# Cross-attention and a top-2 expert layer on one core: the opening put in another order, and the end done in two halves of the tokens

## What is computed

```python
x = x + attention(layernorm(x), ctx, ctx, mask)   # x 1 x 1024 x 128, ctx 1 x 6404 x 128, 16 heads of 8
    # q, k, v with weights and biases; scores / sqrt(8); where(mask, lowest float, scores); softmax; Wo, bo
x = x + ffn(layernorm(x))
    # logits = x @ gate_w.T; softmax; top 2 of 8 experts;
    # per expert h = gelu(x @ w1 + b1), y = h @ w2 + b2; sum of the two, weighted by their probabilities
# mask[b, s, s2] is True for keys 0 .. len-1 of every row: most keys are hidden, those behind len are seen
```

## Time and profile before

| | us |
|---|---|
| three runs | 343.9, 342.21, 339.49 |
| their median | 342.21 |
| the profiled execution | 344.7 |
| its span, first to last instruction | 343.0 |
| PE busy | 269.3 (79%) |
| ACT busy | 233.3 (68%) |
| DVE busy | 175.9 (51%) |
| POOL busy | 64.7 (19%) |

### The profile page before, as it was taken

One profiled execution on the slowest core, in us unless ns is written; L12 is line 12 of the kernel. 1 busy time (PEld: TensorE's weight loads), 2 busy tenths in 40 slices (PEclk: granted clock), 3 DMA queues, 4 the chain that ended last, 5 costly groups with the idle time before them and its releaser, 6 DMA issues.

```text
span 343.0 us, 6176 instructions
## 1 busy us (share of the span) xinstructions
PE 269.3 (79%) x1852; PEld 130.0 (38%) x1852; DVE 175.9 (51%) x423; ACT 233.3 (68%) x365; POOL 64.7 (19%) x109
## 2 busy tenths in 40 slices
PE   0488974899999989899999999796476049999950
PEld 0444554413222212121222212124275049999940
DVE  4939984042345353544445353635791316677722
ACT  3449806356799999999999999892588015555520
POOL 8920002000000000000000002101027703444440
PEclk9999965579999999999999999999989559999995
DMA  6999872010010101001010101059801170101104
GB/s 192 375 263 330 336 162 59 0 28 13 2 38 2 38 11 27 16 22 25 13 36 3 38 11 27 11 172 371 152 9 57 47 193 24 33 31 33 33 31 183
DMA packets 33891, 29.57 MB, mean 86 GB/s; under 512 B 15344, under 2 KB 29192, under 8 KB 33744
## 3 DMA queue, kind: packets, MB, share of 16 engines
q1 hardware_dynamic: 32304, 26.41, 26.8%
q0 software_dynamic: 1568, 2.93, 3.0%
HBM read 21.62 MB, written 7.45 MB: 85 GB/s over the span
## 4 chain that ended last, share of the span: by engine, by line
PE 31%; issue 26%; DVE 16%; ACT 14%; SPq 5%; DMA 4%; ACTq 1%; DVEq 1%; POOL 1%; POOLq 0%
PE bank L1188 7%; ACT w2T L955 7%; ACT arenaB L955 7%; PE bank L1177 6%; PE bank L1311 5%; DVE arenaC L501 4%; SPq L301 4%; PE bank L1174 3%; PE bank L1319 3%; DVE arenaB L864 2%; PE bank L1107 2%; SPq L274 1%; DMA arenaA<-ys_dram 1%; PE bank L1023 1%; DMA x_sb<-in_x_dram 1%
## 5 line engine op out<-in xcount | busy, mean ns | idle before, releaser
L683 DVE TENSOR_TENSOR arenaA<-bank,arenaA 128x512 f32<-128x512 f32 x80 | 55.2, 690 | 84.7 <-PE bank L1188 84.6
L955 ACT ACTIVATE arenaB<-bank 128x1024 f32<-128x1024 f32 x80 | 77.8, 1022 | 12.1 <-PE bank L1177 10.2
L955 ACT ACTIVATE w2T<-bank 128x1024 f32<-128x1024 f32 x80 | 76.8, 1028 | 4.9 <-PE bank L1177 3.8
L1177 PE MATMUL bank<-qS,keys 64*128 64x512 bf16 x324 | 63.8, 392 | 10.0 <-ACT w2T L955 5.0
L985 ACT ACTIVATE mask_u<-bank,arenaB 128x128 f32<-128x128 f32 x92 | 26.2, 368 | 38.9 <-PE bank L1311 38.9
L1177 PEld LDWEIGHTS bank<-qS,keys 64*128 64x128 bf16 x324 | 15.5, 93 | 97.5 <-ACT w2T L955 45.0
L1188 PE MATMUL bank<-arenaB,vcur 128*32 128x512 f32 x320 | 43.0, 609 | 1.0 <-DVE vcur L676 0.3
L1188 PE MATMUL bank<-w2T,vcur 128*32 128x512 f32 x320 | 42.6, 605 | 0.0
L382 POOL COPY arenaC<-ctx_sb 128x128 f32 x11 | 3.2, 293 | 154.5 <-PE bank L1111 153.8
L1311 PE MATMUL bank<-arenaB 128*128 128x128 f32 x184 | 27.6, 297 | 1.6 <-DVE arenaB L856 0.9
L445 POOL DMA_INDIRECT ys_dram<-arenaB,mask_u x23 | 21.9, 952 | 35.2 <-DVE arenaB L870 35.2
(11 more groups left out here) (294 smaller groups left out, 320.9 us busy)
## 6 DMA issues: line engine op xcount, KB each, us to landing
mask_u<-in_L_ffn_w_dram SPq DMA_DIRECT2D x2, 2048.0 KB, 10.5
mask_u<-in_mask_BxSxS_bk_dram SPq DMA_DIRECT2D x6, 560.5 KB, 10.7
qS<-qparts_dram SPq DMA_DIRECT2D x4, 448.0 KB
ctx_sb<-in_ctx_dram SPq DMA_DIRECT2D x2, 768.0 KB, 9.5
mask_u<-in_mask_BxSxS_bk_dram SPq DMA_DIRECT2D x6, 240.0 KB, 7.0
keys_in<-kparts_dram SPq DMA_DIRECT2D x40, 32.0 KB
mask_u<-in_mask_BxSxS_bk_dram SPq DMA_DIRECT2D x1, 1121.0 KB, 9.2
xs_dram<-w1T SPq DMA_DIRECT2D x2, 520.0 KB, 16.9
```

What stands on the lines that cost most here:

```text
L683: nc.vector.tensor_tensor(a, bank[:, 4 + k % 2, :], a, ALU.add).then_inc(s["ac"], 1)
L955: nc.scalar.activation(probs[u % 8], bank[:, 2 * (u % 2):2 * (u % 2) + 2, :].rearrange("p a b -> p (a b)"), ACT.Exp, scale=SCALE).then_inc ...
L1177: last = mm(bank[:, 2 * (u % 2) + a, :], keys[rows, g, :], qS[rows, g, cols], start=not hides, stop=True, tile_position=(64 * a, 0))
```

## The change

**Opening, first part.** GpSimd's first instructions stand in another order; two loads that are needed late are issued later. The memset of `rowkey` waits until the variance step of the layernorm is done (`ln` 5). The layernorm itself has two small steps fewer before its result: factors are folded into scalar_tensor_tensor forms. ACT loads the table with the square root at the start. PE transposes the first context chunk ahead of the queries.

**Opening, second part.** The second and third part of the queries are made by GpSimd (a copy and a subtraction of 128x1024) in place of ACT and DVE. DVE does three of the ORs of the first lot ahead of `qres`. The maxima of the norms are taken in three pieces, and with them the bound up to the product of the norms stands ahead of the last fold; the last three operations of the bound stand in between the steps of the plan. The bias row of the values is copied earlier.

**First tile.** DVE, which has the plan already, copies `cT` in place of GpSimd. PE reads all three of its plan numbers right behind the first projection, ahead of the mask's transposes; before it read `n` ahead of the projection, `general` behind the transposes, and `partial` behind the first scores. The 24 selection matmuls write banks 4 and 5, ACT copies the keys out in two halves of four head pairs, and the hiding matmuls of the first two scores stand between, since their banks are free now.

**End.** The scattered results come back in four loads of 256 KB, first the first four of each partition's eight tokens of both choices, then the others. DVE adds and SP writes each half of the tokens by itself.

```diff
-            sp.dma_start(back[0].rearrange("p (t d) -> p t d", d=D), ys_dram[0:S, :].rearrange("(p t) d -> p t d", t=QT)).then_inc(s["acc0"], 16)
-            sp.dma_start(back[1].rearrange("p (t d) -> p t d", d=D), ys_dram[S:2 * S, :].rearrange("(p t) d -> p t d", t=QT)).then_inc(s["acc1"], 16)
-            sp.wait_ge(s["fin"], 2)
-            sp.dma_start(out.rearrange("a (p t) d -> p (a t) d", t=QT), x2).then_inc(s["outs"], 16)
-            sp.wait_ge(s["outs"], 16)
+            for hf in range(2):
+                ts = slice(4 * hf, 4 * hf + 4)
+                for k in range(2):
+                    sp.dma_start(back[k].rearrange("p (t d) -> p t d", d=D)[:, ts, :],
+                                 ys_dram[k * S:(k + 1) * S, :].rearrange("(p t) d -> p t d", t=QT)[:, ts, :]).then_inc(s["acc1" if hf else "acc0"], 16)
+            for hf in range(2):
+                ts = slice(4 * hf, 4 * hf + 4)
+                sp.wait_ge(s["fin"], 2 * hf + 2)
+                sp.dma_start(out.rearrange("a (p t) d -> p (a t) d", t=QT)[:, ts, :], x2[:, ts, :]).then_inc(s["outs"], 16)
+            sp.wait_ge(s["outs"], 32)
...
+            pool.wait_ge(s["ln"], 5)
             nc.gpsimd.memset(rowkey, -1.0).then_inc(s["rowkey"], 1)
...
-            pool.wait_ge(s["cc_sb"], CHUNKS)
+            pool.wait_ge(s["q_sb"], 2)
+            nc.gpsimd.tensor_copy(qparts[:, 1, :], qres).then_inc(s["q_sb"], 1)
+            pool.wait_ge(s["q_sb"], 3)
+            nc.gpsimd.tensor_tensor(qparts[:, 2, :], qres, qparts[:, 1, :], ALU.subtract).then_inc(s["q_sb"], 1)
             pool.wait_ge(s["plan_ready"], 1)
-            first = pool.value_load(plan[0:1, 0:1], min_val=0, max_val=T - 1)
-            nc.gpsimd.tensor_copy(cT[:, :], ctx_sb[:, bass.ds(first, 1), :].rearrange("p a d -> p (a d)")).then_inc(s["cb"], 1)
...
-            step(nc.vector.tensor_scalar(mean, mean, 1.0 / D, None, ALU.mult))
-            step(nc.vector.tensor_tensor(xout, xin, mean.rearrange("p (t a) -> p t a", a=1).broadcast_to([P, QT, D]), ALU.subtract))
+            step(nc.vector.scalar_tensor_tensor(xout, col(mean), -1.0 / D, xin, ALU.mult, ALU.add))
...
-            step(nc.vector.tensor_scalar(t1, t1, 0.5, None, ALU.mult))
             step(nc.vector.reciprocal(inv, t1))
-            nc.vector.tensor_tensor(xout, xout, inv.rearrange("p (t a) -> p t a", a=1).broadcast_to([P, QT, D]), ALU.mult).then_inc(done, 1)
+            nc.vector.scalar_tensor_tensor(xout, xout, 2.0, col(inv), ALU.mult, ALU.mult).then_inc(done, 1)
+            nc.vector.tensor_scalar(t1, t1, 0.5, None, ALU.mult).then_inc(done, 1)
...
+            dve.wait_ge(s["pad"], 1)
+            ors(0, 1, 2)
             dve.wait_ge(s["rowkey"], len(COMBOS) + 4)
             nc.vector.tensor_scalar(pick, rowkey, iota_p[:, :], None, ALU.is_equal).then_inc(s["pick"], 1)
+            ors(0, 2, 4)
             dve.wait_ge(s["qk_sb"], 1)
             dve.wait_ge(s["q_sb"], 1)
             nc.vector.scalar_tensor_tensor(qres, qp, qk_col[:, 0:1], qparts[:, 0, :], ALU.add, ALU.subtract).then_inc(s["q_sb"], 1)
-            dve.wait_ge(s["pad"], 1)
-            ors(0, 1, QT)
-            dve.wait_ge(s["q_sb"], 3)
-            nc.vector.tensor_tensor(qparts[:, 2, :], qres, qparts[:, 1, :], ALU.subtract).then_inc(s["q_sb"], 1)
+            ors(0, 4, QT)
             folds(0)
...
+            dve.wait_ge(s["kn_ps"], 8)
+            nc.vector.tensor_reduce(nmax[:, 1, :], sizes[:, 0:32, :].rearrange("p t h -> p h t"), axis=AX.X, op=ALU.max).then_inc(s["bd"], 1)
+            ors(1, 1, QT - 1)
+            dve.wait_ge(s["kb_ps"], 1)
+            nc.vector.tensor_copy(bv_all[:, :], bank[:, 3, P:2 * P]).then_inc(s["kb_sb"], 1)
             dve.wait_ge(s["kn_ps"], CHUNKS)
             nc.vector.tensor_reduce(nmax[:, 0, :], sizes[:, T:T + QT, :].rearrange("p t h -> p h t"), axis=AX.X, op=ALU.max).then_inc(s["bd"], 1)
-            nc.vector.tensor_reduce(nmax[:, 1, :], sizes[:, 0:T, :].rearrange("p t h -> p h t"), axis=AX.X, op=ALU.max).then_inc(s["bd"], 1)
+            nc.vector.tensor_reduce(nmax[:, 2, :], sizes[:, 32:T, :].rearrange("p t h -> p h t"), axis=AX.X, op=ALU.max).then_inc(s["bd"], 1)
+            ors(1, QT - 1, QT)
+            dve.wait_ge(s["bd_ps"], 1)
+            nc.vector.tensor_reduce(norms[:, 0:1], bank[0:H, 2, 0:P], axis=AX.X, op=ALU.max).then_inc(s["bd"], 1)
+            nc.vector.tensor_reduce(norms[:, 1:2], bank[0:H, 2, P:3 * P], axis=AX.X, op=ALU.max).then_inc(s["bd"], 1)
+            dve.wait_ge(s["bd"], 5)
+            nc.vector.tensor_tensor(norms[:, 2:3], norms[:, 0:1], norms[:, 1:2], ALU.mult).then_inc(s["bd"], 1)
             folds(1)
-            dve.wait_ge(s["kb_ps"], 1)
-            nc.vector.tensor_copy(bv_all[:, :], bank[:, 3, P:2 * P]).then_inc(s["kb_sb"], 1)
...
+            nc.vector.tensor_tensor(plan[0:1, 66:67], b6[0:1, 129:130], bound[:, 4:5], ALU.add).then_inc(s["plan_ready"], 1)
 
             dve.wait_ge(s["plan_ready"], 1)
-            dve.wait_ge(s["kb_sb"], 1)
             tile0 = dve.value_load(plan[0:1, 0:1], min_val=0, max_val=T - 1)
+            dve.wait_ge(s["cc_sb"], CHUNKS)
+            nc.vector.tensor_copy(cT[:, :], ctx_sb[:, bass.ds(tile0, 1), :].rearrange("p a d -> p (a d)")).then_inc(s["cb"], 1)
...
             n = dve.value_load(plan[0:1, 64:65], min_val=1, max_val=T)
+            general = dve.value_load(plan[0:1, 65:66], min_val=0, max_val=1)
+            dve.wait_ge(s["kb_sb"], 1)
...
+            for hf in range(2):
+                ts = slice(4 * hf, 4 * hf + 4)
+                dve.wait_ge(s["acc1" if hf else "acc0"], 32)
+                nc.vector.tensor_tensor(x2[:, ts, :], x2[:, ts, :], back[0].rearrange("p (t d) -> p t d", d=D)[:, ts, :], ALU.add).then_inc(s["fin"], 1)
+                dve.wait_ge(s["fin"], 2 * hf + 1)
+                nc.vector.tensor_tensor(x2[:, ts, :], x2[:, ts, :], back[1].rearrange("p (t d) -> p t d", d=D)[:, ts, :], ALU.add).then_inc(s["fin"], 1)
...
+            act.wait_ge(s["bd"], 7)
+            nc.scalar.activation(bound[:, 1:2], bound[:, 0:1], ACT.Sqrt, scale=1.02).then_inc(s["bd_sqrt"], 1)
+            nc.scalar.preload_act_table(ACT.Exp)
...
+            for hf in range(2):
+                act.wait_ge(s["k0_ps"], hf + 1)
+                nc.scalar.activation(keys[:, 4 * hf:4 * hf + 4, :].rearrange("p g k -> p (g k)"), bank[:, 4 + hf, :], ACT.Identity, bias=shift_col[:, :]).then_inc(s["kc"], 1)
...
+            pe.wait_ge(s["bd"], 3)
+            for a in range(3):
+                last = nc.tensor.transpose(bank[0:H, 2, a * P:(a + 1) * P], nmax[:, a, :], ident[:, :])
+            last.then_inc(s["bd_ps"], 1)
...
+            for t in range(4):
+                own_logits(t)
+            pe.wait_ge(s["bd"], 6)
+            mm(bank[0:1, 4, 0:H], norms[:, 2:3], ident[0:H, 0:H], start=True, stop=True).then_inc(s["bd_ps"], 1)
+            for t in range(4, QT):
+                last = own_logits(t)
...
             project(0, s["cb"], s["kv"], True)
             pe.sem_inc(s["mt"], 1)
+            pe.wait_ge(s["plan_ready"], 1)
+            n = pe.value_load(plan[0:1, 64:65], min_val=1, max_val=T)
+            general = pe.value_load(plan[0:1, 65:66], min_val=0, max_val=1)
+            partial = pe.value_load(plan[0:1, 66:67], min_val=0, max_val=T)
             pe.wait_ge(s["qk_sb"], 2)
             mask_turn(0)
-            general = pe.value_load(plan[0:1, 65:66], min_val=0, max_val=1)
...
+            pe.wait_ge(s["bias"], 3)
             for gg in range(G):
                 for part in range(3):
                     at = (part * G + gg) * P
-                    last = mm(bank[:, gg // 4, gg % 4 * P:(gg % 4 + 1) * P], pick[:, at:at + P], kparts[:, part, :], start=(part == 0), stop=(part == 2))
-            last.then_inc(s["k0_ps"], 1)
+                    last = mm(bank[:, 4 + gg // 4, gg % 4 * P:(gg % 4 + 1) * P], pick[:, at:at + P], kparts[:, part, :], start=(part == 0), stop=(part == 2))
+                if gg % 4 == 3:
+                    last.then_inc(s["k0_ps"], 1)
+            pe.wait_ge(s["mc"], 1)
+            hide(0, 0)
+            hide(1, 0)
             pe.wait_ge(s["qr"], 64)
             pe.wait_ge(s["qzero"], 32)
             pe.wait_ge(s["kc"], 2)
-            pe.wait_ge(s["mc"], 1)
-            scores(0, 0, 0, 0, True)
-            scores(0, 1, 1, 0, True)
+            products(0, True)
+            products(1, True)
+            pe.wait_ge(s["kc"], 3)
```

174 lines of the change are left out of this document (80 added, 94 removed).

## The result

The changed kernel took 343.26 us, the median of 20 executions, against 341.97 us for 20 of the kernel before; the ratio is 1.0048 (95% interval 1.0029 to 1.0068). Two of the 20 executions took 1292.93 and 1292.71 us, and the ratio leaves them out (experiment 12). Forecast were 337.0 us and a range of 334.3 to 341.0. Later, twelve more executions gave 342.47 us, ratio 1.0020 (0.9991 to 1.0049).

A forecast was written before the change was run, and what follows sets the result against it. The opening was taken as a chain of engines in turn, DVE the limit from 22.6 to 47.7. Terms 2.25 + 0.35 + 0.65 - 1.3 + 1.3 + 1.7 + 0.3 = 5.25 gave 339.5, less 2.5: 337.0 us, range 334.3 to 341.0.

The forecast's parts named there:

- Second lot and the norms: Last context piece lands at 32.9, last norms 40.4, last fold ends 45.4 instead of 47.65: gain 2.25 us.
- what would show me wrong: Long GpSimd subtraction or ORs, changed branch, mask pieces landing at other times because GpSimd's loads moved, PE pausing for queries.
- First mask lot: Last OR waits for its mask piece, landing at 29.5; folds end at 35.0, gain 3.9 us.
- GpSimd against VectorE: Query parts: GpSimd's two instructions may hold DVE's fourth and fifth OR, making the folds 1.2 us later.
- Layernorm, plan, copy of `cT`: Ahead of the first projection: layernorm 2.75 us shorter, bound operations behind the plan 0.35 us, tile copy by DVE 0.65 us.
- PE's loads: Between first projection and branch: three register loads instead of one lose 1.3 us; the branch keeps its 3.54 us.
- Keys in halves and clock: First scores and values: PE's pause goes, gain 1.3 us; the clock may rise earlier, worth 2.8 us, taken as 1.7.
- End: Kernel's end: additions of half the width and a shorter store gain 0.3 us, between -0.5 and 0.9.
- The 2.5 us that I then took off: From profiled execution to median: the three runs' median lay 2.5 us below it, so 339.5 became 337.0 us.
- The landings hold the opening: Rival, chance 0.20: GpSimd holds DVE, context a little later, clock does not move; gain about 2.5 us, 339.7 us.
- The early clock: Rival, chance 0.17: clock rises in the selection's second half and PE's loads cost nothing; gain 7.6 us, 334.6 us.
- starved: Rival, chance 0.03: DVE wins each meeting, GpSimd's query parts wait through ORs and folds; 345 to 349 us.

The follow-up runs named there:

- experiment 12: Changed kernel with plan thresholds making all 51 tiles count as hidden in part, 1343.88 us; with only fully hidden tiles kept, 1278.68 us.
- experiment 1: Changed kernel with four GpSimd loads (b2, broadcast bo, two qS constant rows) issued behind the query parts: 337.83 us, ratio 0.9845.
- experiment 2: Changed kernel with only the two qS constant-row loads issued behind the query parts: 338.41 us, ratio 0.9894.
- experiment 3: The kernel before with the two qS constant-row loads issued behind the query parts: 342.44 us, ratio 1.0015.
- experiment 4: Changed kernel with the last context piece issued ahead of the last three mask pieces of the first lot: 343.27 us, ratio 1.0053.
- experiment 5: Changed kernel with three, then five, unused matmuls of 512 columns on PE ahead of the wait for the last context piece: 340.36 and 340.28 us.
- experiment 10: Query parts back on ScalarE and VectorE, behind the first lot's folds: on experiment 1's kernel 336.53 us, on the fastest kernel (332.82 us) 337.98 us.
- before_rows_late: The kernel of experiment 3: the kernel before with the two qS constant-row loads behind the query parts, 342.44 us.

## Why the prediction was wrong

The changed kernel against the forecast, at the end of the first values (before 72.9, after 71.65; forecast 67.95 on the clock of the trace of before):

| step | forecast | measured | late by |
|---|---|---|---|
| last fold ends | 45.4 | 49.85 | 4.45 |
| fold to plan ready | 3.53 | 3.59 | 0.06 |
| plan to projection | 1.29 | 1.34 | 0.05 |
| projection to selection | 6.4 | 7.02 | 0.6 |
| selection to second scores' end | 5.85 | 5.4 | -0.45 |
| second scores to end of the first values | 5.5 | 4.45 | -1.05 |

*The step that failed is "Second lot and the norms".* It took the last context piece at 32.9 and 7.45 us from there, both from a trace in which PE came to its data late. The change moved GpSimd's loads, and I wrote mask pieces that land at other times because of them under what would show me wrong, but put no price on it. Measured: the piece lands at 34.5 (1.6 later), and from the landing it takes 10.2 us (2.75 more), because PE, faster than before, idled 3.85 us and lost its clock. That is 4.3 of the 4.45 us. DVE, with its bound now ahead of the last fold, waited 1.8 and 2.5 us for it. Experiments 1 to 4 show that the landings are the cause, 5 that the idle time takes the clock.

*What the change did to the landings.* b2 and `bo_all` moved from the quiet first 3 us into the dense stretch; what that costs is not told (experiment 2). The qS loads were there before too (205 GB/s from 21 to 26), but then the third context piece was already in (9.94 to 21.8), and nobody waited. Why 256 KB hold the engines so long is not shown by a run. The Trainium skill (SBUF — State Buffer, "Door 1: The DMA port swizzle (why `[64,N]` ≈ `[32,N]`)") says that DMA bandwidth depends on how many of 16 ports the partitions reach; these loads touch eight partitions a side. Busy engines at 158 GB/s fit that; no run here took it apart. The two loads are also the only ones that go from SBUF to SBUF and that GpSimd issues in this stretch, which is a rival left untested.

*First mask lot:* right, 35.8 against 35.0; the last OR starts at 30.4, not at 29.5, because its mask piece lands that much later. *GpSimd against VectorE:* not seen in the changed kernel, since the subtraction, and the conversion but for its first 1.2 us, fell into the 3.49 us for which DVE waits for its mask. The 1.2 us are 2.4 once the data are on time (experiments 1 and 10); the rule of the Trainium skill that the prediction weighed (SBUF — State Buffer, "Summary: rules for kernel authors") has the traces of experiments 1 and 10 for it: beside GpSimd's two instructions the two ORs took 2.00 and 3.10 us, without them 1.36. *Layernorm, plan, copy of `cT`:* right within 0.1. *PE's loads:* 1.4 measured, 1.3 forecast; but I let the branch keep its 3.54, and it is a fetch, which took 3.88 and 2.35 in two executions. *Keys in halves and clock:* right mechanisms, 0.5 and 1.0 larger than I took. *End:* 0.3, as forecast.

*The second failure is the step from one execution to the median.* The table's sum of 3.7 us explains 343.35 instead of 339.5. The 2.5 us that I then took off, because the execution of before lay that much above its median, were not there for the changed kernel, whose profiled execution lies on its median. The offset goes with the clock. In the twelve executions of before_rows_late it is 340.0 us at a mean granted clock of 0.933 and 344.4 at 0.919, with most at 0.928 (one, 342.7 at 0.915, is out of line); of the kernel before, measured beside the experiments, four executions at 0.919 took 343.7 to 344.8 us and 36 at 0.928 took 339.7 to 343.1. The profiled one was at 0.919. The changed kernel's first executions have 0.900 to 0.928. I take it that in most executions of the kernel before the clock comes up earlier than in its trace, so that part of my 1.7 us for the clock was already in its median; only their mean clock is on record, so this is not shown.

*The rivals.* "The landings hold the opening" named the right place, but its last fold, 1.6 us earlier than before, lies at 46.05, 3.8 ahead of the measured one: it kept the clock of that stretch and the landings as they were. Its terms also add up to 2.9, not to 2.5, so it stood for 339.3. The early clock did not come: the clock stayed at 0.50 up to 67.5, behind the second scores, and the loads cost 1.4. GpSimd was not starved, its subtraction took 2.13 us; the 25 us that I estimated from parts to queries are 24 in experiment 10, from 33.8 to 58. That a change which speeds up the engines ahead of a landing loses the clock while it waits was no rival of mine.

## What to carry to other kernels

When an edit makes engines reach a transfer earlier than before, list who issues what ahead of that transfer on every queue, the unimportant loads too, and price both the landing and the idle time in front of it: on PE it can cost twice, as here, where what followed ran at half clock. First move traffic that nobody waits for out of the stretch; changing the order of what is needed only moved the wait here. And take a single execution's distance from its median as uncertain for both kernels, above all where the clock's rise falls into the stretch that is changed.

## What the runs showed of the hardware

- Two loads of 128 KB from eight partitions onto eight took the DMA engines from 388 GB/s (experiment 2) to 158 over 5 us, at the same busy share; in the other traces of kernels that have them there it is 134 to 216.
- PE's branch over the general case took 0.36 to 0.47 us where the next 16 KB of instructions had been fetched 3.9 us or more ahead of it, 2.3 to 3.9 where the fetch began near its start. Twelve more instructions ahead of it made the difference, 1.7 us up to the selection, so an edit anywhere in PE's stream may do the same.
- PE's clock fell behind idle times of 3.85, 4.50 and 2.90 us in front of the context piece and of 3.18 us in front of the queries, and held behind 0.19; ten small matmuls in its waits were worth up to 3.1 us.
- A GpSimd subtraction of 128x1024 took 2.13 us alone and 3.12 beside ORs, which took 2.00 and 3.10 instead of 1.36. Its conversion to bfloat16 took 2.10 in both traces, but in both an OR ran beside its first 1.2 us, so its time alone is not known.
